# Factors carried inside the scattered rows of a graph kernel, and update and next products in one stage

## The reference, cut to what matters

```python
x = layernorm(x + net0(x))      # 4 layers of: m = silu(silu([h_src, h_dst] @ w1 + b1) @ w2 + b2)
                                # agg = segment_sum(m, src); h += silu([h, agg] @ m1 + c1) @ m2 + c2
x = layernorm(x + attention(x, edge_attr_64, edge_attr_9))
x = layernorm(x + net2(x, edge_attr_16))    # one layer of edge messages, summed by dst
x = layernorm(x + conv(x))                  # normalised sum of neighbours by dst

# the attention, per edge:
wk = relu(edge_attr_64 @ k_w1 + k_b1) @ k_w2 + k_b2     # 128 numbers: the factors of the key
wv = relu(edge_attr_64 @ v_w1 + v_b1) @ v_w2 + v_b2     # 128 numbers: the factors of the value
k, v = (sum over s of edge_attr_9[:, s] * (x_src @ C[:, s])) * wk, ... * wv
attn = sum over 16 of q[dst] * k                        # 8 heads; softmax over a node's edges, then v summed
```

## Time and profile before

| | us |
|---|---|
| three runs | 12512.99, 12523.31, 12532.43; median 12523.31 |
| profiled execution | 12525.73 |
| its span, first to last instruction | 12523.9 |
| busy: PE | 9274.0 (74%) |
| busy: POOL | 8101.0 (65%) |
| busy: DVE | 5811.6 (46%) |
| busy: ACT | 1419.6 (11%) |
| DMA | 1141.33 MB in 818,891 packets |

### The profile page before, as it was taken

The page is one execution under the profiler, slowest core; times in us unless marked ns, Lnnn a source line. Parts: engine busy times, 40 slices in busy tenths (PEclk is TensorE's granted clock), DMA queues, the critical chain, the costliest instruction groups (busy, mean ns, idle before and its releaser), DMA issues. The chain is left out here.

```text
span 12523.9 us, 184074 instructions
## 1 busy us (share of the span) xinstructions
PE 9274.0 (74%) x46241; PEld 7382.7 (59%) x46242; DVE 5811.6 (46%) x14093; ACT 1419.6 (11%) x2535; POOL 8101.0 (65%) x8276
## 2 busy tenths in 40 slices
PE   3777888777677767776777899999993558785333
PEld 1665444566566656665666677777763547674333
DVE  9773000344344434443444455555557754443333
ACT  0002333111111111111111000000000001110000
POOL 3777777777477747774776577776760007775776
PEclk6557889677777777777777899999995658886555
DMA  1333443222222222222222687777772212221111
GB/s 56 102 109 124 142 136 129 65 52 52 40 65 52 52 54 52 52 52 42 52 52 41 169 205 204 205 204 204 203 190 60 87 44 64 64 63 30 26 26 26
DMA packets 818891, 1141.33 MB, mean 91 GB/s; under 512 B 245286, under 2 KB 442294, under 8 KB 817332
## 3 DMA queue, kind: packets, MB, share of 16 engines
q1 hardware_dynamic: 367186, 610.56, 17.7%
q0 software_dynamic: 277888, 340.47, 13.0%
q10 hardware_dynamic: 173666, 188.57, 4.6%
HBM read 939.74 MB, written 199.09 MB: 91 GB/s over the span
## 5 line engine op out<-in xcount | busy, mean ns | idle before, releaser
L1086 POOL DMA_INDIRECT gx_l<-xr,gi_l x4160 | 4007.4, 963 | 2579.8 <-DVE gi_l L1170 1314.5
L1575 PE MATMUL psum<-cw,xa 128*128 128x256 f32 (+1 forms) x8320 | 2116.0, 397 | 0.0
L1575 PEld LDWEIGHTS psum<-cw,xa 128*128 128x128 f32 (+1 forms) x8320 | 1442.6, 189 | 611.7 <-issue 482.4
L1192 DVE TENSOR_TENSOR aggT_l<-aggT_l,psum 64x128 f32 x4160 | 1158.6, 279 | 865.3 <-DVE aggT_l L1192 727.7
L1243 PE MATMUL psum<-ptab,oht 128*128 x6656 | 1176.6, 351 | 378.1 <-issue 204.5
L1243 PEld LDWEIGHTS psum<-ptab,oht 128*128 128x128 f32 x6656 | 1116.0, 262 | 477.4 <-issue 476.0
L1204 DVE TENSOR_TENSOR pre_s_l<-psum,gx_l 128x512 f32<-128x512 f32 x520 | 359.6, 691 | 1988.2 <-DMA gx_l<-xr,gi_l 1929.6
L1563 POOL DMA_INDIRECT wkv<-wtab,ei x832 | 908.5, 1092 | 453.4 <-issue 364.1
L706 POOL DMA_INDIRECT slots_s<-rec_s,row_s x806 | 812.2, 1008 | 399.9 <-issue 395.7
L1556 POOL DMA_INDIRECT gx<-xr,gi x832 | 788.4, 948 | 373.4 <-issue 252.9
L2133 POOL DMA_INDIRECT gx_l<-xr,gi_l x832 | 797.1, 958 | 332.8 <-issue 237.1
(11 more groups left out here) (341 smaller groups left out, 11934.1 us busy)
## 6 DMA issues: line engine op xcount, KB each, us to landing
shb<-shT SPq DMA_DIRECT2D x1872, 128.0 KB
kr<-keyrow_s SPq DMA_DIRECT2D x416, 256.0 KB
gx_l<-xr,gi_l POOLq DMA_INDIRECT x4992
wtab<-eo ACTq DMA_DIRECT2D x152, 512.0 KB, 4.0
vtab<-kv ACTq DMA_DIRECT2D x208, 256.0 KB, 2.4
v_in<-vtab SPq DMA_DIRECT2D x104, 512.0 KB, 3.3
hT<-noderow SPq DMA_DIRECT2D x101, 512.0 KB
kr<-keyrow_d SPq DMA_DIRECT2D x208, 128.0 KB
```

Source lines behind the costliest of these rows:

```text
L1086: pool.indirect_dma_start(gx[j][:, c_, :], None, xr, bass.IndirectOffsetOnAxis(ap=gi[j][:, c_:c_ + 1], axis=0)).then_inc(rows_in[j].sem, 16)
L1192: ins = dve.tensor_tensor(a, a, sums(j, h), ALU.add)
L1575: ins = pe.matmul(bank[2 + p][:, t % 2 * OKV:(t % 2 + 1) * OKV], xa[j][0:n_, c, t * P:(t + 1) * P], cw[0:n_, c, :], start=c == 0, stop=c = ...
```

## The change

Rows of slots_d become WD = 256 + 28 floats, 1,136 bytes: the factors wk and wv of the edge, then the fields (the edge number is gone). The factor turns now follow the edges' layout: a turn is four columns of all partitions, so ein is loaded as partitions 0 to 126 and a tail (one partition); the 128 x 1,024 results stay in eo (a ring of four), DVE adds the fields beside them (`records_dve`), and POOL scatters from eo, four DMAs a turn. wtab, its stores and its gathers go. The logits load the rows of a group in order with one DMA on ACT's queue. Only tiles past column 806 and each block's last tile are filled with empty rows (`pattern_d_sp`, `ends_sp`, 25 DMAs at run-time offsets). slot_rows is now a separate table of the fields alone, written from chunk. PSUM of the second factor product is doubled, and the factor loops are written out in full.

Node transposes, h and layer 0's products (`first_products`) move ahead of the scatter stage: they stand between the sort and the first `features_sp`. After each edge stage one `node_stage` does update and, chunk by chunk, the next layer's products (in the last layer: the output and its addition to x). The barrier after an edge stage is gone (except in net2). Weights, feature stores and the stores of slot_rows move into SP's queue behind its third key load of the edge stage; the load of the next chunk moves to ACT's queue at turn 5; chunk copies and transposes stand at the start of the edge stage. `scatters_end` waits before layer 0. The layer norm after the output comes ahead of the copies of the keys "d".

The diff, cut to its core:

```diff
 OKV = 2 * H * HD
-F_OTHER, F_KEY, F_EDGE, F_SH, F_ATTR = 0, 1, 2, 3, 3 + S
+F_OTHER, F_KEY, F_SH, F_ATTR = 0, 1, 2, 2 + S
 F_NODE = F_ATTR + A
 FD = F_NODE + 1
+WD = OKV + FD
 CHUNK = -(-TILES["d"] // (2 * (LAYERS - 1) * GT)) * GT
 SD = S * D
 KC = -(-SD // P)
...
         for o in "sd":
-            slots[o] = dram(f"slots_{o}", [TILES[o] * P, 2 if o == "s" else FD])
+            slots[o] = dram(f"slots_{o}", [TILES[o] * P, 2 if o == "s" else WD])
             keyrow[o] = dram(f"keyrow_{o}", [TILES[o] * P], BF16)
             gidx[o] = sb(f"gidx_{o}", [P, TILES[o]], I32)
             key[o] = sb(f"key_{o}", [P, TILES[o]])
             blk[o] = sb(f"blk_{o}", [1, -(-TILES[o] // (PER[o] * P)) * P], I32)
-        eid = sb("eid", [P, TILES["d"]], I32)
         xn = sb("xn", [P, NB, D])
         xT = sb("xT", [D, NPAD])
...
         def pattern_d_sp():
+
             sp.wait_ge(patterns.sem, patterns.n)
             sp.nop(nofuse=True)
-            for h in range(4):
-                filled_d.at(sp.dma_start(slot_rows[:, h * FILLED * FD:(h + 1) * FILLED * FD],
-                                         rows_d[:].rearrange("p j c r -> p (j c r)")[:, 0:FILLED * FD]), 16)
+            filled_d.at(sp.dma_start(wide_rows[:, EC:TILES["d"], :], pattern[:].unsqueeze(1).broadcast_to([P, TILES["d"] - EC, WD])), 16)
+
+        def ends_dve():
+            step(dve.tensor_scalar(tile_ends[:], gend[0:1, :], -1.0, 0.0, ALU.add, ALU.max))
+
+        def ends_sp(at):
+
+            sp.wait_ge(done.sem, at)
+            sp.wait_ge(filled_d.sem, filled_d.n)
+            sp.nop(nofuse=True)
+            for b in range(0, NB, CH):
+                last = nc.values_load_multi_w_load_instructions(
+                    tile_ends[0:1, b:b + CH], engines=[sp.engine], min_val=0, max_val=TILES["d"] - 1,
+                    skip_runtime_bounds_check_because="a block's last tile lies before the end of the table")[1]
+                for t_ in last:
+                    filled_d.at(sp.dma_start(wide_rows[:, bass.ds(t_, 1), :], pattern[:].unsqueeze(1)), 16)
...
-                    act.dma_start(ein[j][:], edge_rows(ea64, k, 0)).then_inc(e_loaded[j].sem, 16)
...
-                    act.dma_start(edge_rows(wtab, k, 5), eo[j][:]).then_inc(e_stored[j].sem, 16)
...
+        def first_products():
+            product_weights_sp(0)
+            edge_weights_sp(0)
+            node_weights_sp(0)
+            dve.wait_ge(w1_in.sem, w1_in.n)
+            split_bias(b2r[:], b2[:], b2w)
+            pe.wait_ge(w1_in.sem, w1_in.n)
+            meet()
+            node_products(hcur, hT, w1)
+            sp.wait_ge(w2_in.sem, w2_in.n)
+            sp.nop(nofuse=True)
...
+        def first_column(i):
+            return min(i * EW, EC - EW)
...
+            for i in range(nf):
+                j, c0 = i % AHEAD, first_column(i)
+                pool.wait_ge(e_out.sem, i + 1)
+                pool.wait_ge(rec_in.sem, i + 1)
+                pool.nop(nofuse=True)
+                for t in range(i * EW - c0, EW):
+                    e_gone[j].at(pool.indirect_dma_start(
+                        slots["d"], bass.IndirectOffsetOnAxis(ap=row["d"][:, c0 + t:c0 + t + 1], axis=0),
+                        eo[j][:, t, :], None, bounds_check=TILES["d"] * P - 1, oob_is_err=False), 16)
+
...
+        def records_dve(i):
+            j, c0 = i % AHEAD, first_column(i)
+            if i >= AHEAD:
+                rows_gone(dve, i - AHEAD)
+            ring = c0 % (4 * FC)
+            rec_in.at(dve.tensor_copy(eo[j][:, :, OKV:WD], rows_d[:].rearrange("p j c r -> p (j c) r")[:, ring:ring + EW, :]))
+            g = i * EW // FC + 4
+            if g < NG and (g - 3) * FC <= (i + 1) * EW and (g - 3) * FC > i * EW:
+                dve.wait_ge(rec_in.sem, rec_in.n)
+                fields_dve(g)
...
+                    c0 = first_column(i)
+                    act.dma_start(ein[j][0:P - 1, :], ea64[0:(P - 1) * EC, :].rearrange("(p c) f -> p c f", c=EC)[:, c0:c0 + EW, :].rearrange(
+                        "p c f -> p (c f)")).then_inc(e_loaded[j].sem, 16)
+                    tail = min(ETAIL - c0, EW)
+                    if tail > 0:
+                        act.dma_start(ein[j][P - 1:P, 0:tail * D], ea64[(P - 1) * EC + c0:(P - 1) * EC + c0 + tail, :].rearrange(
+                            "(a c) f -> a (c f)", a=1)).then_inc(e_loaded[j].sem, 16)
+                if k.live(5):
+                    i, j = k.i(5), k.buf(5, AHEAD)
+                    lo = 2 + 4 * k.buf(5)
+                    act.wait_ge(e_second.sem, e_second.n + i + 1)
+                    if k.has(5, AHEAD):
+                        rows_gone(act, i - AHEAD)
+                    act.copy(eo[j][:, :, 0:OKV], PS[:, lo * 512:lo * 512 + EW * OKV].rearrange("p (t f) -> p t f", f=OKV)).then_inc(e_out.sem, 1)
+                if k.live(4):
...
+        keys_at, records_at = 40, 44
+        scatter_s_pool()
+        for g in range(4):
+            features_sp(g)
+            fields_dve(g)
+        table_s_sp()
+        for g in range(4, 8):
+            features_sp(g)
+        scatter_d_pool()
+        for i in range(AHEAD):
+            records_dve(i)
+        table_s_dve()
+        table_kept = done.n
+        for i in range(AHEAD, records_at):
+            records_dve(i)
+        factor_pe()
+        factor_act()
+        keys_dve("s", keyt)
+        keys_sp("s", keyt)
+        for g in range(8, NG):
+            features_sp(g)
+        for i in range(records_at, nf):
+            records_dve(i)
+        for x in namesf:
+            sig(x).n += nf
+        for j in range(AHEAD):
...
+                        if k.fixed and k.t == 2 and "sp" in opening:
+                            opening["sp"]()
...
+                    if k.fixed and k.t == 5 and "act" in opening:
+                        opening["act"]()
...
+            def while_edges_sp():
+
+                if l:
+                    features_out_sp(l)
+                    node_weights_sp(l)
+                if not last:
+                    product_weights_sp(l + 1)
+
...
+            def while_edges_act():
+                if not last:
+                    chunk_in_act(l + 1)
+
+            def sums_first():
+                step(dve.memset(aggT[:], 0.0))
+
...
+            def chunk_first():
+                chunk_dve(l)
                 chunk_pe(l)
                 chunk_act(l)
...
+                first_of_two(0)
+                first_of_two(1)
                 for i in range(NCH):
+                    second_of_two(i)
+                    if i:
+                        products(i - 1)
+                    if i + 2 < NCH:
+                        first_of_two(i + 2)
+                products(NCH - 1)
...
-                chunk_in.at(sp.dma_start(chunk[h][:, 0:w, :].rearrange("p t r -> p (t r)"), slot_rows[:, t0 * FD:(t0 + w) * FD]), 16)
+                chunk_in.at(act.dma_start(chunk[h][:, 0:w, :], wide_rows[:, t0:t0 + w, OKV:WD]), 16)
...
+                rows_out.at(sp.dma_start(slot_rows[:, t0 * FD:(t0 + w) * FD], chunk[h][:, 0:w, :].rearrange("p t r -> p (t r)")), 16)
...
-                if k.live(1):
-                    i, j = k.i(1), k.buf(1)
-                    upto(pool, "ei1_set", k, 1)
-                    upto(pool, "kv1", k, 1, 2)
-                    pool.nop(nofuse=True)
-                    for t in range(GT):
-                        pool.indirect_dma_start(wkv[j][:, t, :], None, wtab, bass.IndirectOffsetOnAxis(ap=ei1[j][:, t:t + 1], axis=0)).then_inc(wrows_in[j].sem, 16)
...
+                if k.live(2):
+                    i, j = k.i(2), k.buf(2)
+                    upto(act, "kv0", k, 2, 2)
+                    upto(act, "kv1", k, 2, 2)
+                    act.nop(nofuse=True)
+                    act.dma_start(wkv[j][:], wide_rows[:, bass.ds(i * GT, GT), :]).then_inc(wrows_in[j].sem, 16)
```

More of the change, by code:

```diff
@@ L660, in build @@
         offsets_dve("d")
+        ends_dve()
+        ends_set = done.n
         blocks_pe("d")
@@ L1048, in node_products, with h_pe, h_act @@
             meet()
-        def edge_messages(o, local, feature=None):
+        def h_pe():
+            for i in range(NCH):
+                if i:
+                    pe.wait_ge(evicted.sem, evicted.n + i)
+                for k in range(2):
+                    ins = pe.matmul(bank[k][:, 0:HALF], w_in[:], xT[:, i * CHN + k * HALF:i * CHN + (k + 1) * HALF], start=True, stop=True)
+                ins.then_inc(product.sem, 1)
+        def h_act():
+            for i in range(NCH):
+                act.wait_ge(product.sem, product.n + i + 1)
+                act.activation(hT[:, i * CHN:(i + 1) * CHN].rearrange("p (k n) -> p k n", k=2), halves(0), ACT.Identity,
+                               bias=b_in[:, 0:1]).then_inc(evicted.sem, 1)
@@ new lines, in build @@
+        h_pe()
+        h_act()
+        product.n += NCH
+        evicted.n += NCH
+        meet()
+        first_products()
+        nf = -(-EC // EW)
```

(47 more changed lines are left out.)

600 lines of the change are left out of this document (277 added, 323 removed).

## The result

The changed kernel takes **13,036.6 us** (median of 4, 13,029.9 to 13,041.7) against 12,527.9 for the kernel before: ratio 1.0407, 95% interval 1.0389 to 1.0425. Forecast were 13,120 (12,900 to 13,450), slower with 0.89.

What follows compares the result with a forecast made beforehand. POOL's 1.28 us per indirect DMA bounds scatter and edge stages, PE the logits. Scatter stage +752, layer 0 start -16, seams -124, ahead of logits -10: +602 on 12,525.7, less 2.4, gives 13,120 (12,900 to 13,450).

Steps and rivals of the forecast that it cites:

- One engine for 127 partitions: Scatter stage: a 127-partition load goes through one DMA engine, so ein's 130,048 bytes take 5.4 us a turn at 24 GB/s.
- The same engine for both queues: Scatter stage: SP's feature loads and ACT's ein loads share one engine; with separate engines the time would be 12,698.
- The sum of 1,855 us: Scatter stage, one engine's work: ein 1,095, features 427, its share of the scatters 333 us; last scatter at 2,997, +752.
- the 12.4 GB/s of the 116-byte rows: Scatter stage, slow end for the wide rows' rate: the scatters' share takes 591 us instead of 333, +258.
- POOL's 1.28 us and the hidden rest of the turn: Scatter stage: POOL's 1.28 us per scatter stays; ACT's and PE's work, 5.6 us a turn, hides below the engine's 9.2.
- Rival 3: Scatter stage: ACT's standing still doesn't hide (+185), or wide rows store slowly (+258): 13,305 to 13,380; chance 0.10.
- The first scatter: Start of the scatter stage: POOL waits for four groups and some 10 ein turns, from 1,214 to about 1,310.
- Seams: Three seams between layers: shorter by 47, 40 and 37 us, -124 in all.
- the node stage: In the seams between layers: five chunks of matmuls take 53 us at the low clock, 27 at the full; 43 taken.
- Ahead of the logits: Stretch before the attention's logits, 120.1 us: output merged into the last node stage, -10, ends -25 and +5.
- Logits 0: Logits: fewer gathers and new loads lie beside a PE at 99%, so 0; ends -18 and +20 us.
- chunk loads 0: Edge stages: chunk loads in 112-byte pieces block ACT up to 22 us, over before POOL needs them: 0, ends 0 and 3 x 25.

Runs made afterwards that it cites:

- Runs 1 to 3: Changed kernel with 127-partition loads cut into 112 and 15: ein and features 12,350.8 us, ein alone 12,385.6, features alone 12,689.9.
- run 5: Kernel before with its 128-partition ein load issued as 127 partitions plus one, three tries: 17,045 against 16,809, 17,195 against 16,993, 17,038 against 16,810 us.
- Experiment 3: Changed kernel with only the feature loads cut into 112 and 15 partitions, ein left at 127: 12,689.9 us.
- experiment 1: Changed kernel with ein and feature loads of 127 partitions cut into 112 and 15: 12,350.8 us against 12,507.0 for the kernel before.
- experiment 6: Kernel before with only its feature loads cut into 112 and 15 partitions: 16,808.4 us against 16,809.5 for the kernel before.
- experiments 6 and 8: Kernel before with features cut 112 + 15: 16,808.4 us; changed kernel with ein cut 126 + 1, features 124 + 3: 15,498.7 us.

## Why the prediction was right, step by step

**One engine for 127 partitions, for ACT's ein too: right.** Runs 1 to 3 show it, run 5 in the kernel before.

**The same engine for both queues: right.** Rows told of it (ein late beside features; the prediction calls them stores, but the earlier trace rows has ein's loads), none named it. Experiment 3 gives 340 us for taking the features off, where separate engines would give 0; and in the changed kernel both queues together move 25 GB/s, with their pieces one after the other.

**The sum of 1,855 us: 74 too high.** Ein's last piece starts at 2895.6 by the trace's packets, 1,781 us after 1115; 14 of the scatters were still to come, so the engine had moved 43.7 MB, at 24.5 GB/s. I had put ein and the features at 24 (34 us too much) and the scatters' share at 22 (35 us too much); the rest are the last 14 scatters, which the sum holds too. Whatever the mix of pieces, the full engine went at 24 to 25 GB/s; the 12.4 GB/s of the 116-byte rows, taken as an end, did not matter. Another 12 us is the start, 1115 and not 1127: the sort ends 9 us earlier than before (1059), and node transposes, h and products take 56 us, not the 58.4 of the earlier trace rows. The pass of the last turn took 19 us, 4 more than the 15 that I had allowed. That is -74 - 12 + 4 = -82, from 2,997 to 2,915.

**POOL's 1.28 us and the hidden rest of the turn: right** (experiment 1, where a turn with everything in it fits under 5.1 us). Rival 3, by which ACT's own work comes on top, had turns of 10.1 us without features; they take 6.98.

**The first scatter**: 1,289, some 1,310 was forecast.

**Seams: 152 us gained, 28 more than forecast.** From the first update matmul to the first gather it is 40.1 us (4006.8 to 4047.0) where I had 49. The step that was mis-sized is the node stage: 34 us (4006.8 to 4041.0) where I took 43. Its rows show the clock rising early:

```profile
4017.71 2.50 PE L1380 MATMUL psum<-z1T,m 128*128 128x320 f32 x4
...
4023.08 1.34 PE L1380 MATMUL psum<-hcur,m 128*128 128x320 f32 x4
...
4024.26 1.28 PE L1396 MATMUL psum<-w,hT 128*128 128x128 f32 x10
```

From 4020 us on the granted clock is the high level, 2.4 GHz: three of five chunks and all products run at it, and ten products take 1.28 us, where I had 2.5 at the low clock. The granted clock of the seams is 0.74 to 0.77 now, 0.63 to 0.68 before.

**Ahead of the logits: 10 forecast, 1 measured.** The merged stage did gain: first update matmul to last addition 46.9 us (7369.5 to 7416.4) for 54.3. What follows gave it back, 48.1 us (7416.4 to 7464.5) for 41.0:

```profile
7417.28 5.89 ACTq L1595 DMA_DIRECT2D cw<-in_L_gnn_Cqk  x9
...
7423.19 5.80 ACTq L1595 DMA_DIRECT2D cw<-in_L_gnn_Cv  x9
...
7429.02 1.28 ACT L744 ACT_TABLE_LOAD   x1 [20.70 <-issue]
...
7430.57 0.32 DVE L746 RECIPROCAL stat<-stat 128x25 f32<-128x25 f32 x1 [5.82 <-ACT stat L744]
```

The attention's 18 weight loads on ACT's queue used to go out beside the output's products. In the kernel before they were through when the layer norm began at 6912.5:

```profile
6889.70 6.04 ACTq L1412 DMA_DIRECT2D cw<-in_L_gnn_Cqk  x9
...
6895.77 5.79 ACTq L1412 DMA_DIRECT2D cw<-in_L_gnn_Cv  x9
```

The stage that covered them is no longer there, and the layer norm's square root stands behind them: 5.8 of the 7 us. It is the question the prediction asked of other steps and not of this one: what covered an issue, and is the cover still there.

**Logits 0, chunk loads 0: right**, within 1 and 2 us a stage. The wide rows land 4.5 us after their issue in a turn of 11.6.

## What to carry to other kernels

Before a load is moved into a stage that has slack on its bound engine, count what each DMA engine gets and not only the mean share: here the DMA share was 0.29 while one engine was full. A flat transfer rate near 24 GB/s and a small DMA that holds its queue for microseconds are the marks of a load on one engine; a load of 127 partitions plus a rest of 1 can be cut in two (112 + 15, or 126 + 1) at the price of one more issue. And where a small stage is merged away, look at what was issued beside it.

## What the runs showed of the hardware that was not expected

**The clock in two equal starts.** The same node stage ran at 1.2 GHz for its first 13 us behind layer 0, with the full clock from 4020 on, and for 40 us behind layer 3, where PE was busy 44.7 of 47 us:

```profile
7370.00:7417.00 47.00, 44.68 (x110) 23.64 (x108) 9.45 (x17) 3.97 (x5) 0.00 (x0) 0.57 0.00 0
```

What PE did just ahead is alike in both, the last groups of an edge stage (busy 8.3 of the 16.8 us ahead at a granted clock of 0.70, and 13.5 of 24 us at 0.71). Why one gets its clock 27 us later is open.

**Groups of runs in which the kernel before took 16,809 to 16,993 us.** Three of the five groups of experiments were such. One chip gave 16,810 in one group and 12,511 in a later one, so it isn't the chip alone. In these groups the queues of SP and ACT move next to nothing while POOL issues indirect DMAs. The DMA view of 400 to 1200 us of the kernel of experiment 6:

```profile
GB/s 1 1 1 1 1 1 1 1 1 1 1 1 1 1 1 1 1 1 1 1 1 1 1 1 1 1 1 1 1 1 1 1 1 1 1 1 1 1 1 1
...
q0 software_dynamic: 18144, 0.62, 1.9%
```

and of 400 to 1000 us of the kernel before in an undisturbed run, SP's queue of the same sort beside the same scatters:

```profile
q1 hardware_dynamic: 23790, 64.96, 37.8%
```

POOL's own DMAs go on at 1.28 us there; the sort hardly proceeds until they end. The form with cut loads gains 7 to 8% in such a group and 1.3% elsewhere. Between the kernels of experiments 6 and 8 (1,310 us apart), 783 us of it are gained before layer 0's first gather (3,495 for 4,278 us), where both kernels issue the same number of indirect DMAs, and some 450 in the logits (2,369 for 2,819 us from POOL's first gather to its last), where it issues 832 fewer. The cause is unknown. No verdict above rests on a comparison across groups.
